# GRU recurrence on TensorE: single-pass products of split operands in place of fp32 products

## The chip, the cores and the metric

The kernel runs on one core of a Trainium2 chip. The metric is the device time of one execution in microseconds (us). The core's engines work side by side and meet at semaphores: PE (TensorE, matmuls; its weight loads are listed as PEld), DVE (VectorE), ACT (ScalarE), POOL (GpSimd) and SP (SyncE, which issues the DMAs).

## The reference, cut to what matters

The whole program is a GRU over 32 time steps, an attention over its states, a residual, then a scan of 32 Runge-Kutta steps with a quantized feed-forward layer on each state, and a second residual. The change touches the GRU. The state h has 128 rows (the batch) and 256 features; each step adds the recurrent products `h @ W_hh` (256 to 768) to the input products:

```
def cell(h, x):
    gi = x @ W_ih + b_ih
    gh = h @ W_hh + b_hh
    i_r, i_z, i_n = jnp.split(gi, 3, axis=-1)
    h_r, h_z, h_n = jnp.split(gh, 3, axis=-1)
    r = jax.nn.sigmoid(i_r + h_r)
    z = jax.nn.sigmoid(i_z + h_z)
    n = jnp.tanh(i_n + r * h_n)
    h_new = (1.0 - z) * n + z * h
    return (h_new, h_new)
_, hs = jax.lax.scan(cell, initial_state, xs)
```

`hs` then goes through the q, k and v projections of the attention. x is (128, 32, 256), in fp32.

## The kernel before, in words

Everything is held transposed: 256 features are two blocks (k) of 128 partitions, and the 128 batch rows are the columns. A gate of 256 features is two output blocks (m) of 128 partitions, so one gate of one step takes 2 x 2 products of a 128x128 weight block with 128 columns of h.

Each engine has its own program, written out by hand, and runs it in that order. The engines meet at semaphores that count (`wait_ge`, `then_inc`); nothing is planned or reordered by a scheduler.

*TensorE* (function `tensor`, the loop at L328). In step t it waits for the h of the step before (`s_h`), runs the gates r, n and z as fp32 products (L337), 12 matmuls in all, each gate into a PSUM bank of its own with a semaphore at its end, and then up to five units of side work (`bulk_unit`, L287 to L315): three units of the input products of the next pair of steps ("gi") and two of the q and k projections of the pair before ("qk"). Side work is done for two steps at once, so it has 256 columns. It uses split operands: a value v is held as a rounded part `v_hi` in the type F32R and a remainder `v_lo = v - v_hi` in the same type, and a product is the sum of three: (lo, hi), (hi, lo) and (hi, hi), two k blocks each, six matmuls a unit (L312 to L314). The six input units of steps 0 and 1 are plain fp32.

*DVE* (function `vector`, L859 to L913), in each step: adds the input part to r (L881), multiplies n's product by the sigmoid of r (L885), adds n's input part (L889), adds z's (L891), forms z*h (L893) and (1-z)*n (L895), and adds these to the new h (L899, semaphore `s_h`). Then it moves the two finished qk units out of PSUM (L856) and rounds one step of x for later input products (L913).

*ACT* (function `scalar`, L634 to L649): sigmoid of r, tanh, sigmoid of z and of -z, up to three outputs of finished gi units, and at the end of the step the rounded part `h_hi` of the new h (L649, semaphore `s_hi`). *POOL* (function `gpsimd`, L1203 to L1216): copies h into the history `hb` that the attention reads (L1208), forms `h_lo` for the qk units (L1211, semaphore `s_hlo`) and `x_lo` (L1215).

The new h alternates between two buffers (`g_h`), h_hi and h_lo between two pairs of steps. The GRU's weights W_hh lie in `wrk` (`whh_s`), loaded in three parts, one per gate. Before the first matmul of the program and in other places `keep_warm` runs matmuls whose results are not used.

Of the kernel before, what the change touches and what calls it, by code (L numbers as in the profile page):

```python
# [6 lines left out]
F32 = mybir.dt.float32  # L7
# [3 lines left out]
ALU = mybir.AluOpType  # L11
# [32 lines left out]
def build(nc, xT, condT, wih, whh, bih, bhh, wq, wk, wv, wo, bqkvo, coupT, cbias, wgT, wuT, wdT, out):  # L44
# [16 lines left out]
    with ExitStack() as ctx:  # L61
        def sb(name, shape, dt=F32):
            return ctx.enter_context(nc.sbuf_tensor(name, shape, dt))

        def sem(name):
# [21 lines left out]
        wmean = sb("wmean", [128, 4])  # L87
        wscale = sb("wscale", [128, 4])
        mag = sb("mag", [128, 2])
        big = sb("big", [128, 8256])  # L90

        kp = lambda d: d.rearrange("(k p) n -> p k n", p=128)
        halves = lambda a: a.rearrange("p (k n) -> p k n", k=2)
# [30 lines left out]
        v_hi, v_lo = ([cut(at, 1024), cut(at + 2048, 1024)] for at in (0, 1024))  # L124
        wv_hi, wv_lo, wo_hi, wo_lo = cut(5120, 512), cut(5632, 512), cut(8192, 512), cut(8704, 512)
        f_hi, f_lo = ([a] * 7 + [b] for a, b in ((cut(6144, 1024), v_hi[0]), (cut(7168, 1024), v_lo[0])))
        Vs = [big[:, 1024 * r:1024 * (r + 1)].rearrange("p (g n) -> p g n", g=4) for r in range(2)]
        PT = [big[:, 2048 + 2048 * r:4096 + 2048 * r].rearrange("p (u n) -> p u n", u=16) for r in range(2)]
        Sc, Sm, Ee, Pn = (big[:, 6144 + 512 * i:6656 + 512 * i].rearrange("p (u n) -> p u n", u=16)
                          for i in range(4))  # L130
        mx, sm, ri = (big[:, 8192 + 16 * i:8208 + 16 * i] for i in range(3))
        banks = PS[:, 0:4, :].rearrange("p g n -> p (g n)").rearrange("p (u n) -> p u n", u=16)
        feats = [PS[:, 5:7, :]] * 7 + [PS[:, 3:5, :]]
        bc = lambda v: v.rearrange("p (u o) -> p u o", o=1).broadcast_to([128, 16, 32])
# [63 lines left out]
        s_r, s_n, s_z = sem("s_r"), sem("s_n"), sem("s_z")  # L198
        s_ar, s_u, s_v, s_az, s_a, s_h = (sem(n) for n in ("s_ar", "s_u", "s_v", "s_az", "s_a", "s_h"))
        s_sr, s_tn, s_sz, s_so = sem("s_sr"), sem("s_tn"), sem("s_sz"), sem("s_so")  # L200
        s_hi, s_hb, s_hlo, s_hlo31 = sem("s_hi"), sem("s_hb"), sem("s_hlo"), sem("s_hlo31")
# [84 lines left out]
        def tensor(pe):  # L286
# [38 lines left out]
            for u in first:  # L325
                bulk_unit(u)
            pe.wait_ge(ld_cond, 16)
            for t in range(T):  # L328
                hprev = g_h[(t - 1) % 2] if t else cond
                if t:  # L330
                    pe.wait_ge(s_h, t)
                for bank, m0, done in ((0, 0, s_r), (1, 4, s_n), (2, 2, s_z)):
                    if t == 0:
                        pe.wait_ge(ld_whh[m0 // 2], 16)
                    for m in range(2):
                        for k in range(2):
                            r = pe.matmul(PS[:, bank, m * 128:(m + 1) * 128],  # L337
                                          whh_s[:, k, (m0 + m) * 128:(m0 + m + 1) * 128], hprev[:, k, :],
                                          start=k == 0, stop=k == 1)
                    r.then_inc(done, 1)  # L340
                for u in at_step[t]:
                    bulk_unit(u)

# [3 lines left out]
            for u in last:  # L347
# [7 lines left out]
            pe.wait_ge(s_hlo, T - 1)  # L355
            pe.wait_ge(s_hlo31, 1)
            for u in last:
                w, m = divmod(u[2], 2)
                for k in range(2):
# [262 lines left out]
        def scalar(ac):  # L622
# [6 lines left out]

            ac.wait_ge(s_const, 1)  # L630
            ac.activation(wsum[:, 3:4], ones[:, 0:1], ACT.Sigmoid)
            for u in first:
                gi_out(u)
            for t in range(T):  # L634
                gis = [u for u in at_step[t] if u[0] == "gi"]
                hn = g_h[t % 2]
                ac.wait_ge(s_ar, t + 1)
                ac.activation(g_r, g_r, ACT.Sigmoid).then_inc(s_sr, 1)  # L638
                ac.wait_ge(s_v, t + 1)
                ac.activation(g_u, g_u, ACT.Tanh).then_inc(s_tn, 1)  # L640
                ac.wait_ge(s_az, t + 1)
                ac.activation(g_z, g_az, ACT.Sigmoid).then_inc(s_sz, 1)
                ac.activation(g_o, g_az, ACT.Sigmoid, scale=-1.0).then_inc(s_so, 1)
                for u in gis[:2]:
                    gi_out(u)
                for u in gis[2:]:
                    gi_out(u)
                ac.wait_ge(s_h, t + 1)
                ac.activation(raw(h_hi[t // 2 % 2][:, :, t % 2 * B:(t % 2 + 1) * B]), hn, ACT.Copy).then_inc(s_hi, 1)  # L649
            ac.wait_ge(s_const, 1)  # L650
            ac.activation(wsum[:, 3:4], ones[:, 0:1], ACT.Exp)
            ac.wait_ge(s_hb, T)
# [181 lines left out]
        def vector(ve):  # L834
# [24 lines left out]
            for t in range(T):  # L859
                n, col = t // 2, t % 2 * B  # L860
                gis = gi[:, n % 2, :, col:col + B]
                hfull = g_h[(t - 1) % 2] if t else cond[:, :, :]
                hn = g_h[t % 2]
                qks = [u for u in at_step[t] if u[0] == "qk"]
                if t == 1:
                    ve.wait_ge(ld_wqk, 32)
                    ve.tensor_copy(raw(wqk_hi), wqk_s).then_inc(s_wqk, 1)
                if t in (2, 3):
                    ve.wait_ge(s_wqk, t - 1)
                    ve.tensor_tensor(raw(wqk_lo[:, t - 2]), wqk_s[:, t - 2], wqk_hi[:, t - 2],  # L870
                                     ALU.subtract).then_inc(s_wqk, 1)
# [24 lines left out]
                if t >= 2:  # L896
                    ve.wait_ge(s_hlo, t - 1)
                ve.wait_ge(s_a, t + 1)
                ve.tensor_tensor(hn, two(g_u), two(g_zh), ALU.add).then_inc(s_h, 1)  # L899
                if t < T - 1:  # L900
                    for u in qks:
                        qk_out(u)
                else:
                    hi, lo = (a[1][:, :, B:2 * B] for a in (h_hi, h_lo))
                    qk_out(qks[0])
                    ve.wait_ge(s_hi, T)
                    ve.tensor_tensor(raw(lo), hn, hi, ALU.subtract).then_inc(s_hlo31, 1)
                    qk_out(qks[1])
# [286 lines left out]
        def gpsimd(po_):  # L1195
# [4 lines left out]
                              pattern=[[-1, 128]], channel_multiplier=1).then_inc(s_const, 1)  # L1200
            po_.wait_ge(s_const, 3)
            po_.tensor_copy(identh[:, :], ident[:, :]).then_inc(s_const, 1)
            for t in range(T):  # L1203
                n, col = t // 2, t % 2 * B
                hn = g_h[t % 2]
                hi, lo = (a[n % 2][:, :, col:col + B] for a in (h_hi, h_lo))
                po_.wait_ge(s_h, t + 1)
                po_.tensor_copy(hb[:, :, :, t], hn).then_inc(s_hb, 1)  # L1208
                if t < T - 1:
                    po_.wait_ge(s_hi, t + 1)  # L1210
                    po_.tensor_tensor(raw(lo), hn, hi, ALU.subtract).then_inc(s_hlo, 1)  # L1211
                if n < 14:
                    at = (n + 2) * 256 + col
                    po_.wait_ge(s_xhi, t + 1)
                    po_.tensor_tensor(raw(x_lo[n % 2][:, :, col:col + B]), x_s[:, :, at:at + B],  # L1215
                                      x_hi[n % 2][:, :, col:col + B], ALU.subtract).then_inc(s_xlo, 1)  # L1216

            po_.wait_ge(s_hlo31, 1)
            po_.wait_ge(s_hlo, T - 1)
# [104 lines left out]
```

## Time and profile before

| | |
|---|---|
| median of 2 runs | 633.4 us (632.79 to 634.02) |
| profiled execution | 632.75 us, of which the span of the trace is 630.8 us |
| PE busy over the span | 590.7 us (94%) |
| PE weight loads (PEld) | 523.7 us (83%) |
| DVE busy | 526.6 us (83%) |
| ACT busy | 404.2 us (64%) |
| POOL busy | 261.5 us (41%) |
| granted TensorE clock | full in all 40 slices of the span |
| recurrent products L337, PE | 744 records of 88.4 us busy, and 24 more with the first state |
| side work L314 of the GRU, split operands, PE | 900 records, 115.6 us busy |

The GRU takes about the first third of the span, the attention the stretch to about 317 us, the scan the rest. A "record" is one TensorE instruction of the trace. Matmuls overlap and their ends are modelled, so the length of one record is longer than the distance between two starts; the cost of one in a dense row is the length of the row divided by the records in it, or the growth of the row with each record. A PE row's "idle before" names who ended the idle time.

### The profile page before, as it was taken

What the parts mean: (1) busy time and instruction counts of PE and PEld (TensorE: products, weight loads), DVE (VectorE), ACT (ScalarE), POOL (GpSimd) and SP (SyncE); (2) the same over time, 40 slices, a digit from 0 to 9 for tenths busy, and PEclk for the clock granted to TensorE, in tenths of its full rate; (3) what the DMA queues carried; (4) which work ended last, traced back from release to release, by engine and by line L of the source; (5) the groups of instructions that cost most, each with busy time, mean ns of one, the idle gap of its engine ahead of it and who ended that gap; (6) DMA issues with size and microseconds to landing.
All of it is one profiled execution on the core that took longest, in us unless ns stands there. A gap on an engine that the chain in (4) does not pass through costs nothing.

```text
span 630.8 us, 14210 instructions
## 1 busy us (share of the span) xinstructions
PE 590.7 (94%) x4918; PEld 523.7 (83%) x4918; DVE 526.6 (83%) x1544; ACT 404.2 (64%) x968; POOL 261.5 (41%) x401
## 2 busy tenths in 40 slices
PE   8899999999999889898879999999999999999997
PEld 7899999999999788787767778777777777777775
DVE  3777777677777588889889999999999999999996
ACT  2554545454544564674467887878778778787775
POOL 0423232323231544221344545555555555555540
PEclk9999999999999999999999999999999999999999
DMA  8400000000000001300000000000000000000000
GB/s 267 159 2 2 1 2 2 1 2 2 1 1 1 18 2 64 118 1 2 1 0 3 18 10 18 16 13 17 11 19 17 11 18 17 11 19 9 19 19 33
DMA packets 12518, 14.87 MB, mean 24 GB/s; under 512 B 1633, under 2 KB 10145, under 8 KB 12449
## 3 DMA queue, kind: packets, MB, share of 16 engines
q1 hardware_dynamic: 12448, 13.97, 6.5%
q8 instruction: 40, 0.66, 0.4%
q14 instruction: 30, 0.24, 0.1%
HBM read 9.78 MB, written 4.19 MB: 22 GB/s over the span
## 4 chain that ended last, share of the span: by engine, by line
PE 68%; ACT 14%; DVE 12%; issue 3%; SPq 1%; DMA 1%; POOL 0%; ACTq 0%; DVEq 0%
PE PS L452 23%; PE PS L314 16%; PE PS L337 12%; ACT q_s L762 4%; PE PS L506 4%; PE PS L528 3%; PE PS L373 2%; ACT q_s L802 2%; ACT k_s L741 2%; ACT big L673 2%; PE PS L430 2%; PE PS L390 2%; DVE big L942 1%; PE PS L490 1%; PE PS L404 1%
## 5 line engine op out<-in xcount | busy, mean ns | idle before, releaser
L452 PE MATMUL PS<-k_s,h_s 128*128 128x128 f32 x1024 | 163.8, 288 | 8.8 <-ACT k_s L741 2.9
L452 PEld LDWEIGHTS PS<-k_s,h_s 128*128 128x128 f32 x1024 | 131.6, 191 | 32.8 <-DVE PS L1034 10.6
L314 PE MATMUL PS<-part 128*128 128x256 f32 x900 | 115.6, 286 | 0.8 <-issue 0.8
L314 PEld LDWEIGHTS PS<-part 128*128 128x128 f32 x900 | 109.8, 191 | 1.0 <-issue 1.0
L741 ACT ACTIVATE k_s<-h_s 128x128 f32<-128x128 f32 x256 | 71.7, 305 | 36.7 <-DVE h_s L1060 32.9
L337 PE MATMUL PS<-big,wrk 128*128 128x128 f32 x744 | 88.4, 275 | 3.0 <-DVE big L899 3.0
L337 PEld LDWEIGHTS PS<-big,wrk 128*128 128x128 f32 x744 | 85.8, 192 | 3.6 <-DVE big L899 3.6
L1208 POOL COPY h_s<-big 128x256 f32<-128x256 f32 x32 | 21.5, 671 | 131.0 <-DVE big L899 131.0
L452 PE MATMUL PS<-h_s 128*128 128x128 f32 x384 | 74.2, 275 | 0.0
L1060 DVE SCALAR_TENSOR_TENSOR h_s<-PS,h_s 128x128 f32<-128x128 f32 x192 | 52.2, 285 | 10.1 <-PE PS L452 7.6
L452 PEld LDWEIGHTS PS<-h_s 128*128 128x128 f32 x384 | 58.3, 192 | 0.0
L638 ACT ACTIVATE big<-big 128x256 f32<-128x256 f32 x32 | 13.4, 418 | 65.6 <-DVE big L881 65.6
L1054 DVE SCALAR_TENSOR_TENSOR h_s<-PS,h_s 128x256 f32<-128x256 f32 x128 | 53.2, 416 | 1.6 <-ACT PS L746 1.1
L746 ACT ACTIVATE PS<-h_s 128x256 f32<-128x256 f32 x128 | 47.8, 373 | 2.9 <-DVE part L948 2.9
L628 ACT ACTIVATE big<-PS,bg 128x256 f32<-128x256 f32 x96 | 41.0, 466 | 6.5 <-DVE bg L838 6.0
L1266 POOL TENSOR_TENSOR h_s<-h_s,k_s 128x256 f32<-128x256 f32 x32 | 25.0, 780 | 42.5 <-DVE q_s L1094 39.7
L1071 DVE SCALAR_TENSOR_TENSOR q_s<-PS,q_s 128x416 f32<-128x416 f32 x64 | 40.8, 640 | 0.6 <-PE PS L554 0.5
L1280 POOL TENSOR_SCALAR h_s<-q_s 128x256 f32<-128x256 f32 x31 | 12.5, 402 | 66.1 <-DVE q_s L1138 66.1
L640 ACT ACTIVATE big<-big 128x256 f32<-128x256 f32 x32 | 13.4, 419 | 38.9 <-DVE big L889 38.9
L1275 POOL TENSOR_TENSOR q_s<-h_s,k_s 128x256 f32<-128x256 f32 x32 | 23.6, 739 | 27.3 <-DVE PS L1040 27.3
L885 DVE SCALAR_TENSOR_TENSOR big<-PS,bh,big 128x128 f32<-128x128 f32 x64 | 19.5, 347 | 18.1 <-ACT big L638 18.1
L762 ACT ACTIVATE q_s<-q_s,mag 128x832 f32<-128x832 f32 x29 | 31.1, 1071 | 0.0
(184 smaller groups left out, 1280.5 us busy)
## 6 DMA issues: line engine op xcount, KB each, us to landing
out<-q_s SPq DMA_DIRECT2D x32, 128.0 KB, 1.7
x_s<-in_xT SPq DMA_DIRECT2D x14, 256.0 KB, 6.2
k_s<-in_wgT SPq DMA_DIRECT2D x1, 832.0 KB, 5.9
k_s<-in_wuT SPq DMA_DIRECT2D x1, 832.0 KB, 7.6
k_s<-in_wih SPq DMA_DIRECT2D x3, 256.0 KB, 4.6
wrk<-in_whh SPq DMA_DIRECT2D x3, 256.0 KB, 4.5
h_s<-in_wdT SPq DMA_DIRECT2D x1, 768.0 KB, 6.4
x_s<-in_xT SPq DMA_DIRECT2D x4, 128.0 KB, 3.8
```

Of the source, the lines that this page charges most:

```text
L314: r = pe.matmul(p, y, x, start=i == 0, stop=i == len(passes) - 1)
L337: r = pe.matmul(PS[:, bank, m * 128:(m + 1) * 128], whh_s[:, k, (m0 + m) * 128:(m0 + m + 1) * 128], hprev[:, k, :], start=k == 0, stop=k == 1)
L452: return pe.matmul(PS[:, m, 0:128], w, x, start=False, stop=True, skip_group_check=True)
L506: r = pe.matmul(po, hqT[0:pk[k], k, :], wd_q[0:pk[k], k, :], start=k == 0, stop=k == NK - 1)
L628: ac.activation(gi[:, n % 2, m, :], bulk_bank(u), ACT.Identity, bias=bg[:, m:m + 1]).then_inc(s_gi, 1)
L741: ac.activation(cm(th[slot % 2], m), cm(src, m), ACT.Tanh).then_inc(s_th, 1)
L746: ac.activation(sqP, src, ACT.Square, scale=math.sqrt(cube[s])).then_inc(s_sq, 1)
L762: ac.activation(hf[:, 0:NI], hN[i % 2], ACT.Identity, scale=h_at(i, 4), bias=mag[:, 0:1]).then_inc(s_hf, 1)
L1054: ve.scalar_tensor_tensor(w_, sqP, cube[s] * own[s], src, ALU.subtract, ALU.mult).then_inc(s_w, 1)
L1060: ve.scalar_tensor_tensor(dst(m), PS[:, m, 0:128], of_ps[slot % 4], cm(w_, m), ALU.mult, ALU.subtract).then_inc(s_next, 1)
L1071: ve.scalar_tensor_tensor(hN[i % 2][:, at], pg[:, g], q_at(i, 3), sg[:, at], ALU.mult, ALU.mult).then_inc(s_hN, 1)
L1266: po_.tensor_tensor(two(W3), two(u3), I_at(t), ALU.add).then_inc(s_W3, 1)
```

## The change

h and the recurrent weights are now used as parts, like the operands of the side work. The gate products of steps 1 to 31 become, for each of the 2 x 2 blocks, three F32R matmuls with 128 columns: lower weights by upper h, upper weights by upper h (`gate_upper`), and upper weights by lower h (`gate_lower`). PE's order in a step is: upper products of r, upper products of n, a wait for the lower h, lower products of r (then `s_r`), lower products of n (then `s_n`), upper and lower products of z (then `s_z`), the side work. Step 0 keeps its fp32 products with the initial state.

The weight parts have a new buffer `whp`; ACT rounds the upper parts before its first step, POOL subtracts for the lower ones. The upper h is written by DVE with an add of its own in front of the add that writes h; the lower h is a DVE subtraction behind it. The ACT rounding and the POOL subtraction of each step go away, and POOL's history copy waits for the lower h. The attention's buffers, which shared the memory of the GRU's, are laid out anew in `big` and a new buffer `sco`.

```
-        big = sb("big", [128, 8256])
+        big = sb("big", [128, 5120])
+        with nc.sbuf_tensor("whp", [128, 3072], F32) as whp:
+            whh_hi, whh_lo = (whp[:, 1536 * i:1536 * (i + 1)].rearrange("p (k n) -> p k n", k=2) for i in range(2))
+        sco = sb("sco", [128, 3136])
...
-            for t in range(T):
-                hprev = g_h[(t - 1) % 2] if t else cond
-                if t:
-                    pe.wait_ge(s_h, t)
-                for bank, m0, done in ((0, 0, s_r), (1, 4, s_n), (2, 2, s_z)):
...
+            def gate_upper(t, bank, m0):
+                hh = h_hi[(t - 1) // 2 % 2][:, :, (t - 1) % 2 * B:((t - 1) % 2 + 1) * B]
+                if t == 1:
+                    pe.wait_ge(s_wlo[m0 // 2], 1)
+                for m in range(2):
+                    for k in range(2):
+                        for w in (whh_lo, whh_hi):
+                            pe.matmul(PS[:, bank, m * 128:(m + 1) * 128],
+                                      raw(w[:, k, (m0 + m) * 128:(m0 + m + 1) * 128]), raw(hh[:, k, :]),
+                                      start=m == 0 and k == 0 and w is whh_lo, stop=False, skip_group_check=True)
+
+            def gate_lower(t, bank, m0, done):
+                hl = h_lo[(t - 1) // 2 % 2][:, :, (t - 1) % 2 * B:((t - 1) % 2 + 1) * B]
+                for m in range(2):
+                    for k in range(2):
+                        r = pe.matmul(PS[:, bank, m * 128:(m + 1) * 128],
+                                      raw(whh_hi[:, k, (m0 + m) * 128:(m0 + m + 1) * 128]), raw(hl[:, k, :]),
+                                      start=False, stop=k == 1, skip_group_check=True)
+                r.then_inc(done, 1)
+
+            for t in range(T):
+                if t == 0:
+                    first_gates()
+                else:
+                    pe.wait_ge(s_hi, t)
+                    gate_upper(t, 0, 0)
+                    gate_upper(t, 1, 4)
+                    pe.wait_ge(s_hlo, t)
+                    gate_lower(t, 0, 0, s_r)
+                    gate_lower(t, 1, 4, s_n)
+                    gate_upper(t, 2, 2)
+                    gate_lower(t, 2, 2, s_z)
...   (scalar)
+            def upper_weights(i):
+                ac.wait_ge(ld_whh[i], 16)
+                ac.activation(raw(whh_hi[:, :, 256 * i:256 * (i + 1)]), whh_s[:, :, 256 * i:256 * (i + 1)],
+                              ACT.Copy).then_inc(s_whi, 1)
...
-                ac.wait_ge(s_h, t + 1)
-                ac.activation(raw(h_hi[t // 2 % 2][:, :, t % 2 * B:(t % 2 + 1) * B]), hn, ACT.Copy).then_inc(s_hi, 1)
...   (vector)
                 ve.wait_ge(s_a, t + 1)
+                ve.tensor_tensor(raw(hi), two(g_u), two(g_zh), ALU.add).then_inc(s_hi, 1)
                 ve.tensor_tensor(hn, two(g_u), two(g_zh), ALU.add).then_inc(s_h, 1)
...
+                ve.wait_ge(s_hi, t + 1)
+                ve.wait_ge(s_h, t + 1)
+                ve.tensor_tensor(raw(lo), hn, hi, ALU.subtract).then_inc(s_hlo, 1)
+                for u in qks:
+                    qk_out(u)
...   (gpsimd)
+            for j, i in enumerate((0, 2, 1)):
+                po_.wait_ge(s_whi, j + 1)
+                po_.tensor_tensor(raw(whh_lo[:, :, 256 * i:256 * (i + 1)]), whh_s[:, :, 256 * i:256 * (i + 1)],
+                                  whh_hi[:, :, 256 * i:256 * (i + 1)], ALU.subtract).then_inc(s_wlo[i], 1)
...
-                po_.wait_ge(s_h, t + 1)
+                po_.wait_ge(s_hlo, t + 1)
                 po_.tensor_copy(hb[:, :, :, t], hn).then_inc(s_hb, 1)
-                if t < T - 1:
-                    po_.wait_ge(s_hi, t + 1)
-                    po_.tensor_tensor(raw(lo), hn, hi, ALU.subtract).then_inc(s_hlo, 1)
```

## Rows read from the trace of the kernel before

**Rows 1.** Stretch 100 to 150 us: busy us of PE, PEld, DVE, ACT, POOL.

```profile
100.00:150.00 50.00, 50.00 (x432) 50.00 (x432) 35.66 (x88) 23.89 (x64) 15.93 (x24) 1.00 0.01 1
```

**Rows 2.** Chain of waits, 98 to 112 us: start us, us, what.

```profile
99.09 2.68 PE PS L337 x24
101.77 3.59 PE PS L314 x30
```

**Rows 3.** Timeline of a steady step: start us, us, engine, line, tiles, count, idle.

```profile
105.20 2.84 PE L337 MATMUL PS<-big,wrk 128*128 128x128 f32 x24
...
106.36 0.42 DVE L881 TENSOR_TENSOR big<-PS,big 128x256 f32<-128x256 f32 x1 [0.17 <-PE PS L337]
...
108.33 0.42 DVE L891 TENSOR_TENSOR big<-PS,big 128x256 f32<-128x256 f32 x1
...
109.23 0.43 DVE L893 TENSOR_TENSOR big<-big 128x256 f32<-128x256 f32 x1 [0.49 <-ACT big L642]
...
109.58 0.42 DVE L895 TENSOR_TENSOR big<-big 128x256 f32<-128x256 f32 x1
110.10 0.42 DVE L899 TENSOR_TENSOR big<-big 128x256 f32<-128x256 f32 x1
...
110.61 0.41 ACT L649 ACTIVATE part<-big 128x256 fp32r<-128x256 f32 x1
...
111.12 0.74 POOL L1211 TENSOR_TENSOR part<-big,part 128x256 fp32r<-128x256 f32 x1
...
111.47 0.72 PE L337 MATMUL PS<-big,wrk 128*128 128x128 f32 x5
```

**Rows 4.** Timeline of the first two steps, and all adds on r (line L881).

```profile
10.54 2.84 PE L337 MATMUL PS<-cond,wrk 128*128 128x128 f32 x24
...
13.99 0.42 DVE L881 TENSOR_TENSOR big<-PS,big 128x256 f32<-128x256 f32 x1
...
14.45 0.42 ACT L638 ACTIVATE big<-big 128x256 f32<-128x256 f32 x1 [3.23 <-DVE big L881]
...
18.13 2.05 PE L337 MATMUL PS<-big,wrk 128*128 128x128 f32 x16 [1.57 <-DVE big L899]
...
19.40 0.42 DVE L881 TENSOR_TENSOR big<-PS,big 128x256 f32<-128x256 f32 x1
...
L881 DVE TENSOR_TENSOR big<-PS,big x32: 410/425/425, 14.0 to 206.4; 128x256 f32<-128x256 f32 x32
```

**Rows 5.** Weight loads: L410's timeline and durations (min/median/max ns), L314's loads.

```profile
265.28 0.28 PE L410 MATMUL PS<-wsum,ones 128*128 128x1 f32 x2
...
265.17 0.31 PEld L410 LDWEIGHTS PS<-wsum,ones 128*128 128x128 f32 x2
...
L410 PEld LDWEIGHTS PS<-wsum,ones x6: 188/190/192, 265.2 to 287.7; 128*128 128x128 f32 x6
L410 PE MATMUL PS<-wsum,ones x6: 164/207/250, 265.3 to 287.7; 128*128 128x1 f32 x6
...
L314 PEld LDWEIGHTS PS<-part x900: 186/192/192, 14.1 to 208.7; 128*128 128x128 f32 x180
```

**Rows 6.** Transposes, one record each: timeline, then groups with mean ns.

```profile
500.50 0.38 PE L545 MATMUL PS<-ident,x_s 128*128 128x128 f32 x2
...
503.30 0.55 PE L490 MATMUL PS<-identh,q_s 128*128 128x128 f16 x7 [0.35 <-ACT q_s L762]
...
L490 PE MATMUL PS<-identh,q_s 128*128 128x128 f16 x203 | 16.0, 218 | 9.8 <-ACT q_s L762 9.8
...
L545 PE MATMUL PS<-ident,x_s 128*128 128x128 f32 x60 | 11.4, 273 | 0.0
```

**Rows 7.** Timeline of the end of the GRU stage.

```profile
210.16 0.42 DVE L899 TENSOR_TENSOR big<-big 128x256 f32<-128x256 f32 x1
...
210.62 0.42 ACT L649 ACTIVATE part<-big 128x256 fp32r<-128x256 f32 x1 [1.05 <-DVE big L899]
...
211.09 2.17 PE L353 MATMUL PS<-part 128*128 128x256 f32 x16 [0.26 <-ACT part L649]
```

More of the change, by code:

```diff
@@ L126, in build @@
         f_hi, f_lo = ([a] * 7 + [b] for a, b in ((cut(6144, 1024), v_hi[0]), (cut(7168, 1024), v_lo[0])))
[L127 to L131, printed above, removed]
+        Vs = [a.rearrange("p (g n) -> p g n", g=4) for a in (big[:, 0:1024], sco[:, 2048:3072])]
+        PT = [big[:, 1024 + 2048 * r:3072 + 2048 * r].rearrange("p (u n) -> p u n", u=16) for r in range(2)]
+        Sc, Sm, Ee, Pn = (sco[:, 512 * i:512 * (i + 1)].rearrange("p (u n) -> p u n", u=16) for i in range(4))
+        mx, sm, ri = (sco[:, 3072 + 16 * i:3088 + 16 * i] for i in range(3))
         banks = PS[:, 0:4, :].rearrange("p g n -> p (g n)").rearrange("p (u n) -> p u n", u=16)
@@ L200, in build @@
         s_sr, s_tn, s_sz, s_so = sem("s_sr"), sem("s_tn"), sem("s_sz"), sem("s_so")
-        s_hi, s_hb, s_hlo, s_hlo31 = sem("s_hi"), sem("s_hb"), sem("s_hlo"), sem("s_hlo31")
+        s_hi, s_hb, s_hlo = sem("s_hi"), sem("s_hb"), sem("s_hlo")
+        s_whi = sem("s_whi")
+        s_wlo = [sem(f"s_wlo{i}") for i in range(3)]
         s_bulk, s_gi, s_qk, s_qka = sem("s_bulk"), sem("s_gi"), sem("s_qk"), sem("s_qka")
@@ L327, in tensor, with first_gates @@
             pe.wait_ge(ld_cond, 16)
-            for t in range(T):
-                hprev = g_h[(t - 1) % 2] if t else cond
-                if t:
-                    pe.wait_ge(s_h, t)
-                for bank, m0, done in ((0, 0, s_r), (1, 4, s_n), (2, 2, s_z)):
-                    if t == 0:
-                        pe.wait_ge(ld_whh[m0 // 2], 16)
+            gates = ((0, 0, s_r), (1, 4, s_n), (2, 2, s_z))
+            def first_gates():
+                for bank, m0, done in gates:
+                    pe.wait_ge(ld_whh[m0 // 2], 16)
                     for m in range(2):
@@ L337, in tensor @@
                             r = pe.matmul(PS[:, bank, m * 128:(m + 1) * 128],
-                                          whh_s[:, k, (m0 + m) * 128:(m0 + m + 1) * 128], hprev[:, k, :],
+                                          whh_s[:, k, (m0 + m) * 128:(m0 + m + 1) * 128], cond[:, k, :],
                                           start=k == 0, stop=k == 1)
                     r.then_inc(done, 1)
+            def gate_upper(t, bank, m0):
[28 more added lines that the diff above has]
+                    gate_lower(t, 2, 2, s_z)
                 for u in at_step[t]:
@@ L354, in tensor @@
                                   stop=False)
-            pe.wait_ge(s_hlo, T - 1)
-            pe.wait_ge(s_hlo31, 1)
+            pe.wait_ge(s_hlo, T)
             for u in last:
@@ L631, in scalar @@
             ac.activation(wsum[:, 3:4], ones[:, 0:1], ACT.Sigmoid)
+            def upper_weights(i):
+                ac.wait_ge(ld_whh[i], 16)
+                ac.activation(raw(whh_hi[:, :, 256 * i:256 * (i + 1)]), whh_s[:, :, 256 * i:256 * (i + 1)],
+                              ACT.Copy).then_inc(s_whi, 1)
             for u in first:
                 gi_out(u)
+            for i in (0, 2, 1):
+                upper_weights(i)
             for t in range(T):
                 gis = [u for u in at_step[t] if u[0] == "gi"]
-                hn = g_h[t % 2]
                 ac.wait_ge(s_ar, t + 1)
@@ L896, in vector @@
                 if t >= 2:
-                    ve.wait_ge(s_hlo, t - 1)
+                    ve.wait_ge(s_hb, t - 1)
+                hi, lo = (a[n % 2][:, :, col:col + B] for a in (h_hi, h_lo))
                 ve.wait_ge(s_a, t + 1)
+                ve.tensor_tensor(raw(hi), two(g_u), two(g_zh), ALU.add).then_inc(s_hi, 1)
                 ve.tensor_tensor(hn, two(g_u), two(g_zh), ALU.add).then_inc(s_h, 1)
-                if t < T - 1:
[L901 to L908, printed above, removed]
+                ve.wait_ge(s_hi, t + 1)
[3 more added lines that the diff above has]
+                    qk_out(u)
                 if n < 14:
@@ L1205, in gpsimd @@
                 hn = g_h[t % 2]
-                hi, lo = (a[n % 2][:, :, col:col + B] for a in (h_hi, h_lo))
-                po_.wait_ge(s_h, t + 1)
+                po_.wait_ge(s_hlo, t + 1)
                 po_.tensor_copy(hb[:, :, :, t], hn).then_inc(s_hb, 1)
-                if t < T - 1:
-                    po_.wait_ge(s_hi, t + 1)
-                    po_.tensor_tensor(raw(lo), hn, hi, ALU.subtract).then_inc(s_hlo, 1)
                 if n < 14:
@@ L1216, in gpsimd @@
                                       x_hi[n % 2][:, :, col:col + B], ALU.subtract).then_inc(s_xlo, 1)
-            po_.wait_ge(s_hlo31, 1)
-            po_.wait_ge(s_hlo, T - 1)
+            po_.wait_ge(s_hlo, T)
             po_.wait_ge(s_hb, T)
```

## The prediction

> **What bounds the kernel now.** I read the views in this order: busy shares by stretch, the chain of waits inside one GRU step, the timeline of that step, and then the rows that tell what one TensorE record costs. The edit sits in the GRU stage; its 32 steps run from the first add on the r gate at 14.0 us to the last at 206.4 us [rows 4]. In that stage PE is busy 50.00 us of 50.00 while DVE has 35.66 and ACT 23.89 [rows 1]. The chain of waits between 98 and 112 us names nothing but PE: 24 records of the recurrent products in 2.68 us, then 30 records of side work (input and q/k products) in 3.59 us [rows 2]. So a step costs 2.68 + 3.59 = 6.27 us, which is also the distance from 105.20 to 111.47, two starts of the recurrent group [rows 3]. A record costs 2.68 / 24 = 0.112 us there and 3.59 / 30 = 0.120 us in the side work.
>
> How much room is beside PE? The last add writes h from 110.10 to 110.53 us, PE takes it at 111.47 [rows 3]: 0.94 us of slack. The first steps, whose side work is 18 records and not 30, show the recurrence bare: adds on r at 13.99 and 19.40 us, 5.41 us apart, with PE idle before it starts at 18.13 [rows 4]. The intervals between the 32 adds on r are 2 of 5.41, 28 of 6.27, and the last one, whose side work is 12 records: 192.4 - 10.8 - 175.6 = 6.0 us.
>
> **The change part by part.** *Recurrent products.* Twelve fp32 matmuls a step, recorded as two records each (24), become 36 single products with 128 moving columns: (low weights, high h), (high, high), (high, low h). I expect one record each, since the side work, in the same number format, has 5 units of 6 products and 30 records. Everything hangs on the price p of one such record, and no row of before shows this format at 128 columns. Bounds from the nearest rows:
>
> - The moving pass alone: seven fp16 transposes with 128 columns take 0.55 us, one record 0.218, so 0.33 / 6 = 0.055 us each [rows 6]. That is the low end.
> - The weight load: a fresh 128x128 block precedes every product. Two fp32 products with a single moving column, nothing to stream, still span 0.28 us where the shortest is 0.164, so the second comes 0.112 us after the first; their two loads, 0.188 to 0.192 us long, span 0.31 [rows 5]. Loads of the side work's format have the same length, 192 ns at the median [rows 5]; the fp16 transposes do not pay it. Two fp32 transposes, one record of 0.273 each, span 0.38, so they are 0.11 us apart too [rows 6].
> - The side work's own pace, 0.120 us at 256 columns: the high end of the simple reading, as half the columns should not cost more.
>
> By the load rows p lies between 0.108 and 0.120; I take 0.115, halfway between the one-column pair and the side work, as the format is the side work's and the width is nearer the pair's. The matmul gets half as long and the load does not: three products of one load each in place of two records of one load each. Group time: 36 x 0.115 = 4.14 us against 2.68, so +1.46 us a step, and PE has no idle time in a steady step to absorb it.
>
> The Trainium skill's page "TensorE: Matmul & The Clock Gate" (LDWEIGHTS) gives a load as columns / 1.2 ns, 107 ns for 128, and its table of weight-path modes says that fast weight load has no win for fp32. By that figure alone the step would be 36 x 0.107 = 3.85 us, the forecast 669; the trace's one-column pair stands 5 ns above it.
>
> *Recurrence.* PE now runs high products of r and n (16), waits for the low part of h, runs 4 + 4 low ones, then z. The r gate is complete after 20 records, not 8: 20 x 0.115 - 8 x 0.112 = +1.41 us before the add on r. z is complete after 36 x 0.115 = 4.14 us, plus 0.28 for the last record's length; its add stood at 108.33 - 105.20 = 3.13 us and would be shifted to 4.54 anyway, so z sets nothing. The bare recurrence is 5.41 + 1.41 = 6.82 us, below the 4.14 + 3.59 = 7.73 us of PE: in steady steps PE stays the bound, with about 0.9 us of slack for h.
>
> *New wait for the low part.* PE's wait stands in front of the 20 remaining gate products and all side work of the step. DVE writes the high part where h was written, then h 0.35 us later (the pace of independent adds, 109.23 to 109.58), the low part 0.52 later again (a dependent add, 109.58 to 110.10), and it ends 0.42 after that [rows 3]: 1.29 us after the start of the high add. PE starts on the high part at about 0.5 at the earliest and spends 16 x 0.115 = 1.84 us on it. Covered by 1.0 us, cost nothing; if PE were bound by h and p were 0.055, the cover would still be 0.1 us.
>
> *DVE.* Two more adds a step, some 0.87 us, ahead of the two q/k outputs. DVE has 14.3 of 50 us idle [rows 1], 1.8 us a step. Its outputs wait for PE's side work in any case. *ACT* loses the rounding copy (0.41 us) and *POOL* the low subtraction (0.74 us) [rows 3]; neither was on the chain, so nothing. POOL's copy of h into the history now waits for the low part, about 0.9 us later than before; DVE reuses h two steps on, nothing.
>
> *Splitting the weights.* Three ACT copies of 512 columns, at most twice the 0.42 us of 256 columns each, stand before ACT's first sigmoid. ACT sits idle for the 3.23 us before 14.45, and the last third of the weights has landed by the time PE begins z without a pause, 10.54 + 16 x 0.112 = 12.3 us [rows 4]. 12.3 + 0.84 = 13.2 is before 14.45: hidden. POOL's three subtractions, at most 1.5 us each, end before 18.13, when step 1 begins: hidden.
>
> *Start, end, storage.* Step 0 keeps its fp32 products. After the last step PE started the final q/k products at 211.09, behind ACT's rounding at 210.62; the high part is now there when h was (210.16 + 0.42) [rows 7]: -0.4 us. The moved attention buffers change no instruction: nothing.
>
> *Sum.* 28 steady intervals x 1.46 = 40.9. The other 3 go by the recurrence: 3 x 1.41 = 4.2. End -0.4. Together +44.7 us on the profiled execution's 632.75 us (span 630.8 and 1.95 around it), which lies 0.65 below the median shown: **677 us**, 1.07 times. With p = 0.108 the sum is 28 x 1.21 + 3 x 1.27 - 0.4 = +37.3, 670 us; with 0.120 it is 28 x 1.64 + 3 x 1.51 - 0.4 = +50, 683 us.
>
> **The rivals.** *Loads hide, the change wins* (the other side). If the array takes a block's weights at no cost beside a 128-column pass, p is 0.055 to 0.065 (the pass, plus the 0.008 by which the side work exceeds two such passes). At 0.060 PE needs 2.16 + 3.59 = 5.75 us, the recurrence 5.41 + 1.20 - 0.90 = 5.71: 0.52 us less in 28 steps, 0.3 more in 3, -0.4: 619 us; 614 to 624 over the span of p. It decides at the weight load before each of the 36 products, from p below 2.68 / 36 = 0.0745. For it: the fp16 pace [rows 6]. Against it: the one-column pair [rows 5]. Chance 0.08, half of it beyond 2%. The same page's issue-gap rule, N / 2.4 + 2.5 ns, would give 56 ns a product and this case; the one-column pair speaks against its use here.
>
> *The format loses its advantage at 128 columns* (the change does not do what it says). Each product costs what an fp32 one does now, two records, 0.224 us: 8.06 + 3.59 = 11.65 us, +5.38 in 28 steps. z ends so late that it sets the other 3: its add moves from 3.13 to 8.06 + 0.28 + 0.09 = 8.43, +5.3. 28 x 5.38 + 15.9 - 0.4 = +166, 799 us. For it: all this format's rows have 256 or 512 columns, none 128. Against: nothing in its rows hints at a second pass. Chance 0.12.
>
> *Load and pass do not overlap for short products*: p = 0.107 + 0.065 = 0.172. PE 6.19 + 3.59 = 9.78, +3.51 in 28; the 3 others by z, +3.4: +108, 741 us. For it: the fp32 transposes, whose pace of 0.11 is a short load plus a short pass. Against: the side work, whose 0.120 holds both side by side. Chance 0.08.
>
> **How the numbers follow.** Forecast 0.72, rivals 0.08, 0.12 and 0.08. The forecast's bounds are 670 to 683; I add 4 below for steps whose DVE work now ends sooner relative to PE. The forecast and the non-overlap rival together hold 0.80, so the range is 666 to 745. What a measurement here can tell from no change is about 2%, 621 to 646 us: faster 0.04, within 0.04, slower 0.92.
>
> **What would show it.** In the changed profile: the high and low gate groups with 36 records a step and PE at 100% in steady steps; 7.7 us between adds on r; starts of gate records 0.11 to 0.12 us apart, loads still 190 ns; PE not idle at the wait for the low part; clock at 1.00. A pace near 0.06 and PE idle before each step would prove the first rival, 72 records or 0.22 us per record the second, 0.17 us the third. A stall of PE before the low products would show my cover wrong.

## The result, and the profile after

The changed kernel takes 681.6 us (median of 2 runs, 680.2 to 682.9) against 633.4 (median of 2 runs): slower, ratio 1.076 with a 95% interval of 1.071 to 1.081. Its profiled execution took 680.17 us, with a span of 678.2 against 630.8.

The same stretch as [rows 1], now of the changed kernel; the columns are busy us of PE, PEld, DVE, ACT and POOL:

```profile
100.00:150.00 50.00, 50.00 (x436) 50.00 (x435) 32.81 (x87) 18.65 (x49) 8.42 (x12) 1.00 0.00 1
```

PE is still busy throughout and everything else is less so. The chain of waits of one steady step answers to [rows 2] (start us, us, what; L353 is the line of the products with the upper h, L361 of those with the lower h, L319 the side work):

```profile
120.65 1.74 PE PS L353 x16
122.39 0.89 PE PS L361 x8
123.28 0.90 PE PS L353 x8
124.17 0.45 PE PS L361 x4
124.62 3.63 PE PS L319 x30
```

36 gate records take 3.98 us, 0.111 us each, where 24 took 2.68, and the side work takes 3.63 us where it took 3.59. The step is 7.61 us and holds nothing but PE. The timeline shows the slack beside it, as [rows 3] did:

```profile
119.07 0.43 DVE L940 TENSOR_TENSOR part<-big 128x256 fp32r<-128x256 f32 x1
119.41 0.42 DVE L941 TENSOR_TENSOR big<-big 128x256 f32<-128x256 f32 x1
119.93 0.43 DVE L944 TENSOR_TENSOR part<-big,part 128x256 fp32r<-128x256 f32 x1
...
120.49 1.90 PE L353 MATMUL PS<-part,whp 128*128 128x128 f32 x16
...
122.22 1.05 PE L361 MATMUL PS<-part,whp 128*128 128x128 f32 x8
```

The upper h (L940) is there at 119.50, 0.99 us before PE takes it, and the lower h (L944) at 120.36, 1.86 us before its first product. No steady step waits for a part of h. PE waits for the upper h only in step 1 (2.3 us) and in step 31 (1.1 us), where the side work before it is short; the kernel before waited there too.

What is not in steady steps stands at the start, against [rows 4]:

```profile
11.98 5.49 POOL L1243 TENSOR_TENSOR whp<-wrk,whp 128x512 fp32r<-128x512 f32 x3 [10.01 <-ACT whp L670]
12.23 2.83 DVE L887 TENSOR_TENSOR part<-k_s,part 128x1536 fp32r<-128x1536 f32 x1
14.99 0.41 DVE L921 TENSOR_TENSOR big<-PS,big 128x256 f32<-128x256 f32 x1
...
16.60 1.15 DVE L929 TENSOR_TENSOR big<-big 128x256 f32<-128x256 f32 x1
...
22.86 0.42 DVE L921 TENSOR_TENSOR big<-PS,big 128x256 f32<-128x256 f32 x1 [0.94 <-PE PS L361]
31.73 0.42 DVE L921 TENSOR_TENSOR big<-PS,big 128x256 f32<-128x256 f32 x1 [1.45 <-PE PS L361]
```

The first add on r comes 1.0 us late, and the first two steps last 7.87 and 8.87 us. In the second, the clock is low; the columns of the next row are as above, then PE's granted clock:

```profile
21.65:28.47 6.82, 6.82 (x34) 6.82 (x34) 3.48 (x10) 2.03 (x5) 0.85 (x1) 0.50 0.05 15
```

Half clock is the 1.2 GHz level. The 20 gate records from 21.70 to 25.96 us start 0.213 us apart, against 0.111 at full clock. Before it PE had been busy only 4.14 of the 6.60 us from 15.00 on. A second such stretch runs from 250.3 to 257.2 us, at the end of the GRU stage.

All adds on r run from 15.0 to 252.0 us:

```profile
L921 DVE TENSOR_TENSOR big<-PS,big x32: 412/425/425, 15.0 to 252.0; 128x256 f32<-128x256 f32 x32
```

**Where the 47.4 us of span are.** Start +1.0; the first two intervals 16.74 against 10.82, +5.9; the 28 steady ones 28 x (7.60 - 6.27) = +37.2; the last 7.42 against 5.99, +1.4; behind the last add 426.2 against 424.4, +1.9.

### The profile page after: what moved, and what is told of

Same layout as the page of the kernel before. It is cut to its first block, busy times and chain, and to the rows that moved or that the text cites. A ratio compares the mean times of both kernels' runs of the same rounds, so it can differ in the third digit from the quotient of the medians.

```text
span 678.2 us, 14992 instructions
## 1 busy us (share of the span) xinstructions
PE 637.7 (94%) x5290; PEld 571.0 (84%) x5290; DVE 543.9 (80%) x1607; ACT 395.9 (58%) x939; POOL 249.0 (37%) x373
## 4 chain that ended last, share of the span: by engine, by line
PE 73%; ACT 13%; DVE 8%; issue 3%; SPq 1%; DMA 1%; POOL 0%; ACTq 0%; DVEq 0%
PE PS L488 21%; PE PS L319 16%; PE PS L353 12%; PE PS L361 6%; ACT q_s L802 4%; PE PS L542 4%; PE PS L564 3%; ACT q_s L842 2%; ACT k_s L781 2%; PE PS L466 2%; PE PS L409 2%; PE PS L426 2%; ACT sco L713 2%; DVE big L980 1%; PE PS L526 1%
## 5 line engine op out<-in xcount | busy, mean ns | idle before, releaser
L319 PE MATMUL PS<-part 128*128 128x256 f32 x900 | 116.4, 287 | 1.6 <-issue 1.6
L319 PEld LDWEIGHTS PS<-part 128*128 128x128 f32 x900 | 111.7, 194 | 1.8 <-issue 1.8
L353 PE MATMUL PS<-part,whp 128*128 128x128 f32 x744 | 93.8, 276 | 3.4 <-DVE part L940 3.4
L353 PEld LDWEIGHTS PS<-part,whp 128*128 128x128 f32 x744 | 90.1, 195 | 3.8 <-DVE part L940 3.8
L361 PE MATMUL PS<-part,whp 128*128 128x128 f32 x372 | 54.2, 283 | 0.0
L361 PEld LDWEIGHTS PS<-part,whp 128*128 128x128 f32 x372 | 49.1, 201 | 0.0
L921 DVE TENSOR_TENSOR big<-PS,big 128x256 f32<-128x256 f32 x32 | 13.6, 425 | 40.3 <-PE PS L361 40.3
```

The source lines that it names most:

```text
L319: r = pe.matmul(p, y, x, start=i == 0, stop=i == len(passes) - 1)
L353: pe.matmul(PS[:, bank, m * 128:(m + 1) * 128], raw(w[:, k, (m0 + m) * 128:(m0 + m + 1) * 128]), raw(hh[:, k, :]), start=m == 0 and k == 0 ...
L361: r = pe.matmul(PS[:, bank, m * 128:(m + 1) * 128], raw(whh_hi[:, k, (m0 + m) * 128:(m0 + m + 1) * 128]), raw(hl[:, k, :]), start=False, s ...
```

## The experiments

All are edits of the changed kernel, and ratios are to the kernel before. Where one experiment's change is built on another's, it says so.

**Is it the load or the pass?** Two runs halve the one and the other. The pass is the streaming of the columns of h, the load is that of the weight block. In the first run each gate product streams 64 columns of h, so half of the batch is left out of the gates:

```
-   pe.matmul(PS[:, bank, m * 128:(m + 1) * 128], raw(w[:, k, ...128 columns]), raw(hh[:, k, :]), ...
+   pe.matmul(PS[:, bank, m * 128:m * 128 + 64],  raw(w[:, k, ...128 columns]), raw(hh[:, k, 0:64]), ...
```

> The 36 gate products of each step stream 64 columns of h in place of 128 (half of the batch's gates are left out); weight blocks, order and waits stay. Theory L (each product pays the load of a fresh 128x128 block, 0.11 us, which the pass of 128 columns hides behind): the records stay 0.111 us apart, a steady step stays at 7.6 us, the time near 680 us (678 to 683). Rival P (at 128 columns the format streams twice, like the fp32 transposes, 2 x 0.055 us): the pace falls to about 0.06, PE needs 36 x 0.06 + 3.63 = 5.8 us, a step 5.7 to 5.9, the time about 627 to 633 us.

Measured: 706.2 us, one execution. Chain of waits of one step:

```profile
117.92 1.71 PE PS L353 x16
119.62 0.89 PE PS L361 x8
120.52 0.89 PE PS L353 x8
121.41 0.45 PE PS L361 x4
```

36 records in 3.94 us, 0.109 each: half the streaming bought nothing, and the steps at full clock stay at 7.61 us. Rival P is out. The time was missed for another reason, which neither theory had: the clock. The next rows are the stretch with these lines and the one after it:

```profile
112.00:122.00 10.00, 10.00 (x89) 10.00 (x89) 6.21 (x17) 3.10 (x8) 1.41 (x2) 1.00 0.00 0
122.20:125.60 3.40, 3.40 (x18) 3.40 (x18) 2.30 (x7) 1.99 (x6) 0.34 (x1) 0.50 0.02 5
```

PE is listed as busy for all of both, with records in the first as dense as in the changed kernel, and yet the grant drops to half for 3.4 us again and again through the GRU stage; the 11 steps in which it does last 9.1 us. Before that it was at half from 19.8 to 43.7 us, and the first three intervals lasted 9.6, 11.5 and 11.3 us. Together these are 24.5 of the 26.0 us by which the span is longer than the changed kernel's. That the narrower pass is what lowers the clock is argued from this one execution; no other run tests it.

In the second run the weight blocks have 64 columns, so half of each gate's outputs are left out, and 128 columns of h pass:

```
-   pe.matmul(PS[:, bank, ...],     raw(w[:, k, (m0 + m) * 128:(m0 + m + 1) * 128]),  raw(hh[:, k, :]), ...
+   pe.matmul(PS[0:64, bank, ...],  raw(w[:, k, (m0 + m) * 128:(m0 + m) * 128 + 64]), raw(hh[:, k, :]), ...
```

> The 36 gate products load weight blocks of 64 columns in place of 128 (half of each gate's outputs are left out) and stream 128 columns of h as in the changed kernel. Theory L: the load halves to about 0.053 us and the pace falls to 0.056 to 0.065 us, a steady step to 5.7 to 5.9 us, the time to about 627 to 633 us. Rival P: the two passes stay, 0.11 us a record, the time near 680 us.

Measured: 636.3 us, one execution. Durations of loads and products (min/median/max ns), and one step:

```profile
L361 PEld LDWEIGHTS PS<-part,whp x372: 133/135/223, 22.1 to 209.4; 128*64 128x64 f32 x186
...
114.66 1.12 PE L353 MATMUL PS<-part,whp 128*64 128x128 f32 x16
...
115.27 1.23 DVE L896 TENSOR_SCALAR k_s<-PS,ba 128x256 f32<-128x256 f32 x2
...
116.33 0.29 DVE L951 CAST part<-x_s 128x256 fp32r<-128x256 f32 x1
...
116.53 0.42 DVE L921 TENSOR_TENSOR big<-PS,big 128x256 f32<-128x256 f32 x1
...
116.71 0.73 POOL L1253 TENSOR_TENSOR part<-x_s,part 128x256 fp32r<-128x256 f32 x1 [0.55 <-DVE part L951]
...
117.58 3.83 PE L319 MATMUL PS<-part 128*128 128x256 f32 x30 [0.59 <-POOL part L1253]
```

The load is 57 ns shorter than the changed kernel's 192, and 16 products take 1.12 - 0.22 = 0.90 us beyond one record's length, 0.06 us each. With the passes untouched, the price per product falls with the load: theory L holds. By columns / 1.2 ns, the Trainium skill, "TensorE: Matmul & The Clock Gate" (LDWEIGHTS), gives 53 ns for a load of 64 columns and 107 for one of 128. The trace agrees with the difference, 57 ns between the loads' records. The pace of 0.06 us is also near that of a pass of 128 columns (0.055, [rows 6]), so it shows that the shorter load costs no more than this, not what it costs by itself.

My time for this run was too low by 3 to 9 us. The step is 6.2 us, not 5.8. I took the cause for POOL: lower h, two q/k outputs, cast of x, POOL's lower x, and only then the side work, before which PE idles 0.59 us; the expectations of the first three fp16 versions below still say so. The chain of waits of this run says otherwise: it holds neither PE nor POOL and goes on DVE from the lower h (L944) over the two q/k outputs (L896, 1.23 us) and the cast (L951) straight to the next add on r (L921), then on between DVE and ACT.

**Is it the number of products?** One of three products is left out, and with it POOL's subtractions:

```
-   for w in (whh_lo, whh_hi):
+   for w in (whh_hi,):
...
-   po_.tensor_tensor(raw(whh_lo[...]), whh_s[...], whh_hi[...], ALU.subtract)
```

> Two products per block and step in place of three (lower weights by upper h is left out), and POOL's three subtractions for the lower weights at the start are gone with it. Theory L: 24 records x 0.111 = 2.67 us, so a step is 2.67 + 3.6 = 6.27 us again: 28 x -1.33 = -37 us and about -4 in the first and last steps; without POOL's subtractions the first add on r is back at 14.0 us and DVE's adds of step 0 at 0.42 us, -1.7. Together 636 to 641 us. Rival W (what costs is the wait for the lower h or the two added DVE operations, not the number of records): a steady step stays above 7 us and the time above 665 us.

Measured: 635.4 us, ratio 1.003 (1.001 to 1.005), 0.6 us below what I expected. One step's gate products in its chain of waits, and of its start the long subtraction and two adds:

```profile
103.21 0.84 PE PS L353 x8
104.05 0.90 PE PS L361 x8
104.95 0.45 PE PS L353 x4
105.39 0.45 PE PS L361 x4
```

```profile
12.45 1.75 DVE L887 TENSOR_TENSOR part<-k_s,part 128x1536 fp32r<-128x1536 f32 x1
14.12 0.41 DVE L921 TENSOR_TENSOR big<-PS,big 128x256 f32<-128x256 f32 x1
...
15.85 0.42 DVE L929 TENSOR_TENSOR big<-big 128x256 f32<-128x256 f32 x1
```

24 records, 2.64 us, and 6.26 us a step: the price of the fp32 version, although the wait for the lower h and DVE's two added operations are all there. (The profile is of the longest of the five executions, 640.5 us; its stretches at half clock lie outside the rows shown.) Rival W is out. DVE's start is back to its old durations once POOL's subtractions are gone.

**One part undone.** The gate products go back to fp32 on h; the rest of the change stays:

```
-   pe.wait_ge(s_hi, t)
-   gate_upper(t, 0, 0)
...
+   pe.wait_ge(s_h, t)
+   (the 12 fp32 products of the kernel before)
```

> The changed kernel with the gate products of steps 1 to 31 put back to fp32 on h itself; everything else of the change stays (DVE writes both parts, POOL and ACT lose theirs, the weights are still split at the start, the attention's buffers stay moved). Theory L: a steady step is 24 x 0.112 + 3.6 = 6.27 us again; what is left is the start, where POOL's subtractions slow DVE (1.0 us before the first add on r, 0.7 in step 0) and perhaps a lower clock in the first steps: 634 to 639 us, ratio to the kernel before 1.002 to 1.008. Rival W: the added DVE operations hold the steps above 6.6 us, 645 us or more.

Measured: 638.4 us, ratio 1.0065 (1.0048 to 1.0082), within what was expected. The chain of waits of a step is that of before:

```profile
100.11 3.59 PE PS L319 x30
103.71 2.68 PE PS L374 x24
```

So of the 7.6% the gate products are 7, and the rest of the change, the start included, is 0.65%.

**The slow start.** POOL starts its subtractions behind DVE's long one:

```
+   po_.wait_ge(s_wih, 2)
    for j, i in enumerate((0, 2, 1)):
        po_.wait_ge(s_whi, j + 1)
```

> The changed kernel, but POOL begins its three subtractions for the lower recurrent weights only when DVE has done its long subtraction for the input weights. Theory S (two-input operations of POOL and DVE that run at the same time slow each other: DVE's subtraction took 2.83 us beside them, 1.75 alone): DVE's subtraction is back at 1.75 us and the first add on r at 13.9 to 14.2 us; the collision moves into step 0, whose adds beside POOL take 0.7 to 1.1 us in place of 0.42, so the total stays within 2 us of the changed kernel's. Rival T (DVE was slow for another reason, the placement of the buffers): 2.8 us and a first add at 15 us as before.

Measured: 682.0 us (2 runs, ratio 1.078, 1.072 to 1.084), as expected. Its start:

```profile
12.56 1.75 DVE L887 TENSOR_TENSOR part<-k_s,part 128x1536 fp32r<-128x1536 f32 x1
14.23 0.42 DVE L921 TENSOR_TENSOR big<-PS,big 128x256 f32<-128x256 f32 x1
14.40 3.95 POOL L1244 TENSOR_TENSOR whp<-wrk,whp 128x512 fp32r<-128x512 f32 x3 [12.43 <-DVE part L887]
...
15.85 1.38 DVE L929 TENSOR_TENSOR big<-big 128x256 f32<-128x256 f32 x1
17.14 0.41 DVE L931 TENSOR_TENSOR big<-PS,big 128x256 f32<-128x256 f32 x1
```

The long subtraction is back at 1.75 us and the collision has moved to L929, 1.38 us in place of 0.42. L931, which has one operand in PSUM, ran at 0.41 while POOL was at work, and so did L921 in the changed kernel. That fits the Trainium skill, "SBUF — State Buffer" (SBUF: two separate sides): DVE and GpSimd have one port pair in common, and the instruction that starts first holds it alone. The traces agree on the order too. In the changed kernel POOL began first (11.98 against 12.23 us) and DVE's long subtraction grew by 1.08 us. In the run with filled idle time, next, DVE began first, kept its 1.75 us beside POOL, and POOL's three took 4.99 us in place of 3.95:

```profile
12.13 1.75 DVE L896 TENSOR_TENSOR part<-k_s,part 128x1536 fp32r<-128x1536 f32 x1
12.71 4.99 POOL L1252 TENSOR_TENSOR whp<-wrk,whp 128x512 fp32r<-128x512 f32 x3 [10.74 <-ACT whp L679]
```

The runs show the slowdown only between operations that have both inputs in SBUF. The first add on r came 0.76 us earlier than in the changed kernel, but the total gained nothing: the second interval was 9.25 us (8.87), and 428.1 us (426.2) passed behind the last add, with a stretch at half clock from 325.5 us among them. So what the start costs is read from the rows, not from a time.

**The clock.** Unused matmuls fill PE's idle time in steps 0 and 30:

```
    for u in at_step[t]: bulk_unit(u)
+   if t == 0:
+       pe.wait_ge(s_ar, 1)
+       keep_warm(0, 9)
+   if t == T - 2:
+       pe.wait_ge(s_ar, T - 1)
+       keep_warm(0, 8)
```

(and six more ahead of step 0's side work)

> The changed kernel with unused matmuls where PE sits idle: 12 records before and 18 behind the side work of step 0, 16 behind that of step 30. Theory C: the granted clock of one half that the changed kernel shows for 6.8 us from 21.6 us and again from 250.3 us comes from the idle PE just before (3.9 us in step 0, some 2 us each in steps 30 and 31) and costs about 2 us each time; filled, the first steps cost 6.8 us, not 8.9, and the time is 676 to 679 us, ratio to the changed kernel about 0.994. Rival D: the lower clock comes from the sparser recurrent products themselves (128 columns for each load), and it stays: 680 to 683 us.

Measured: 678.8 us (674.5 to 680.5), ratio 1.070 (1.065 to 1.075), at the upper edge of theory C's range; its interval overlaps that of the changed kernel. The two stretches that were low before are now whole in the profiled execution, and the second interval is 6.7 us, not 8.9:

```profile
20.00:32.00 12.00, 11.73 (x102) 11.53 (x102) 7.88 (x20) 4.25 (x12) 3.08 (x4) 1.00 0.19 68
240.00:260.00 20.00, 18.86 (x180) 18.56 (x179) 12.84 (x30) 6.84 (x14) 6.57 (x6) 1.00 0.05 15
```

In the profile the direction is shown: the 12 us from 20.00 hold 102 records and not 79. That execution was the fastest of the four, the only one with a mean granted clock of 1.000; the others had 0.995 to 0.997, still above the 0.990 and 0.985 of the changed kernel's two. In the times it is not settled, and what the filling cost elsewhere (the first interval grew to 8.3 us) was not taken apart.

**A version with a cheap load.** If a rounded 32-bit block costs 0.11 us and an fp16 transpose with 128 columns goes at 0.055, the same three products in fp16 parts should be cheap. h, and the recurrent and q/k weights, as fp16 pairs:

```
-   with nc.sbuf_tensor("whp", [128, 3072], F32) as whp:
+   with nc.sbuf_tensor("whp", [128, 3072], FP16) as whp:
...
-   ve.tensor_tensor(raw(hi), two(g_u), two(g_zh), ALU.add).then_inc(s_hi, 1)
+   ve.tensor_tensor(hi, two(g_u), two(g_zh), ALU.add).then_inc(s_hi, 1)
```

> The changed kernel with h and the weights it meets (recurrent, q and k) split into two fp16 parts, not two of the rounded 32-bit format; three products a block as before, same order; the input products keep their format. Theory L: fp16 blocks load in far less than 0.11 us, so a gate product costs 0.056 us and a q/k product 0.109. PE: 36 x 0.056 + 12 x 0.109 + 18 x 0.12 = 5.5 us a step, but the chain that set 6.18 us in the run with half blocks (lower h, q/k outputs, cast of x, POOL's lower x, input products) is as long: steps of 6.0 to 6.2 us, 627 to 633 us. Rival P (128 columns are too short for three products in any format): 0.1 us and more a product, 675 us and up.

Measured: 632.0 us (10 runs), ratio 0.997 (0.996 to 0.999), inside the expected range; the steps are 6.1 us. With x in fp16 parts too:

> As the fp16 version for h, with x and its weights in fp16 parts as well: all 66 products of a step are fp16. Theory L: PE needs 36 x 0.056 + 30 x 0.109 = 5.3 us a step and waits; the chain over POOL's lower x sets the step at 5.9 to 6.1 us: 624 to 630 us. Rival: a step bound by PE would gain the full 0.3 us against the other fp16 version.

Measured: 632.7 us, ratio 0.998 (0.996 to 1.000), above the expected range by 2.7 us, and the steps are 6.1 us again. The cheaper side work brought nothing, so PE is no longer the bound; but my account of what is was not right, as the next one shows. It is built on the version with all products in fp16: the cast of x and POOL's lower x were moved ahead (and the unused matmuls were in):

> All products in fp16 parts, the unused matmuls in steps 0 and 30, and the cast of x moved ahead of DVE's last operations of the step, with POOL's lower x ahead of its history copy. Theory X: what holds the light steps is the chain lower h, q/k outputs, cast of x, lower x, input products; moved out of it, the step falls to the recurrence, 5.41 + 20 x 0.056 - 0.90 = 5.63 us: 28 x -0.64 = -18 us against the kernel before, 615 to 620 us. Rival Y: the added adds on DVE bound the step, and it stays at 6.0 us or more, 626 us and up.

Measured: 635.4 us, ratio 1.003 (1.002 to 1.004). Theory X fell: the cast and POOL's lower x had left the chain, and the step was 6.2 us all the same; rival Y's 626 us and more came true. Its timeline names the cause:

```profile
114.45 1.07 PE L355 MATMUL PS<-p,whp 128*128 128x128 f16 x16 [0.79 <-DVE p L956]
114.83 0.42 DVE L960 TENSOR_TENSOR p<-big,p 128x256 f16<-128x256 f32 x1
115.17 1.16 DVE L907 TENSOR_SCALAR k_s<-PS,ba 128x256 f32<-128x256 f32 x2
...
115.35 0.61 PE L363 MATMUL PS<-p,whp 128*128 128x128 f16 x8
...
116.18 0.40 DVE L932 TENSOR_TENSOR big<-PS,big 128x256 f32<-128x256 f32 x1
...
118.82 0.67 POOL L1262 TENSOR_TENSOR p<-x_s,p 128x256 f16<-128x256 f32 x1 [2.83 <-DVE p L947]
...
119.02 0.75 DVE L949 TENSOR_TENSOR big<-big 128x256 f32<-128x256 f32 x1 [0.28 <-ACT big L695]
```

r's last product, the fourth of the eight from 115.35, ends at about 115.8, but DVE is in the two q/k outputs and gets to the add on r at 116.18. The move also had a price: POOL's lower x now runs beside DVE's z*h (L949), which takes 0.75 us in place of 0.42 (median of 31), 0.33 us a step on the chain. So this run does not show what taking the cast off the chain (0.28 us) is worth; without the collision its step would still be about 5.9 us, an estimate from 6.25 - 0.33, and not theory X's 5.63.

In the PE-bound kernels the outputs lay in DVE's idle time. Now, again from the version with all products in fp16 and without the unused matmuls, they go one step later, one behind the add on r and one behind the add on z, where DVE waits for a sigmoid:

```
    ve.tensor_tensor(two(g_r), two(PR), gis[:, 0:2], ALU.add).then_inc(s_ar, 1)
+   for u in qks[:1]: qk_out(u)
...
+   for u in qks[1:]: qk_out(u)
    ve.wait_ge(s_sz, t + 1)
...
-   for u in qks: qk_out(u)          (behind the lower h)
```

> All products in fp16 parts; the two q/k outputs of a step are taken by DVE one step later, one behind the add on r and one behind the add on z, where DVE waits for ACT's sigmoids, and not behind the lower h; POOL forms the lower x before its history copy. Theory Y (from the run with the cast of x moved: DVE's operations in front of the next add on r, 1.16 us of q/k outputs among them, set the light step): the add on r comes when PE has r, 0.35 us earlier, and a steady step falls from 6.1 - 6.2 to 5.7 - 5.9 us; 28 x -0.45 = -13 us against the kernel before, 1.5 to 3 back for the start: 621 to 626 us. Rival Z (the recurrence itself is 6.1 us long once the parts are formed): no gain against the other fp16 versions, 630 to 634 us.

Measured: 615.3 us (614.5 to 618.8), ratio 0.972 (0.969 to 0.976), 6 us under my range. The add on r again waits for PE:

```profile
115.55 1.07 PE L355 MATMUL PS<-p,whp 128*128 128x128 f16 x16 [0.15 <-DVE p L946]
...
116.45 0.61 PE L363 MATMUL PS<-p,whp 128*128 128x128 f16 x8
...
116.95 0.42 DVE L923 TENSOR_TENSOR big<-PS,big 128x256 f32<-128x256 f32 x1 [0.39 <-PE PS L363]
```

16 products in 1.07 us are (1.07 - 0.22) / 15 = 0.057 each, and the steps are 5.61 us. The two q/k outputs (0.66 us each) end within 0.13 us of the sigmoids for which DVE would wait anyway. The formula of the prediction's first rival, 5.41 + 20 x 0.056 - 0.90, gives 5.63. This is faster than both kernels.

> The same with the unused matmuls in steps 0 and 30. Both theories: the granted clock is full in the GRU stage either way in most runs, so the two differ by less than 2 us; if the version without them shows a stretch at half clock, this one is 1 to 2 us faster.

Measured: 617.7 us, ratio 0.974 (0.971 to 0.977). Its interval overlaps that of the version without the filling, so the filling is worth nothing that shows here.

## Why the prediction was right, and where its terms were off

- **PE is the bound and has no room.** Right: the chain of waits of a steady step is PE alone before and after, and the run with fewer products took back in full what they had cost.
- **The price of a product, the load.** Right in kind, 4% too high in size. I took 0.115 us, halfway between the one-column pair [rows 5] and the side work; it is 0.111, near the pair's 0.112. Over 28 steps that is 40.9 us forecast against 37.2. But I had misread the pair. Its second product starts 0.026 us after the first, not 0.112, and is the longer one (0.250 us after 0.164), so it is their ends that lie 0.112 apart, and their loads start 0.118 apart (265.167 and 265.285 us). The pair pointed at the load, but its nearness to 0.111 is in part luck. The load's part, which I could only argue from it, is shown by the two half runs.
- **Side work, wait for the lower h, slack.** Right: 3.63 us where I had 3.59, in a steady step PE never waits for a part, 0.99 us of slack where I had 0.9.
- **DVE's two adds cost nothing.** Right in this kernel, and shown by the run with two products. It held only under PE's cover: in the light versions DVE's queue was the bound (6.1 us, and 5.61 with the q/k outputs moved). What the two adds alone cost there was not measured.
- **The three intervals by the recurrence.** The working is right, its conditions were not: +4.2 us forecast, +7.4 measured. With the clock whole the second interval was 6.70 us (the run with filled idle time), where 5.41 + 1.41 = 6.82 was forecast. In the changed kernel it was 8.87, about 2.2 us lost at half clock. The first lost 0.7 us to L929 and 0.4 to its four lower products of r at half clock, 4 x (0.213 - 0.111). I had expected the clock at 1.00 throughout.
- **The weights' splitting is hidden.** Wrong: +1.0 us before the first add and 0.7 in step 0. I checked that ACT and POOL were free in time, which they were, but not what POOL's work does to DVE beside it. This is the one term that was put at nothing on a wrong reason; the later start of POOL showed it.
- **The end.** -0.4 us forecast, +1.9 measured: PE came late to the last q/k products, 259.19 us, 1.7 us behind the upper h at 257.50, behind side work and unused matmuls that the half clock had delayed. With the clock whole, in the run with filled idle time, the stretch behind the last add was 423.7 us, -0.7 against the kernel before.
- **The rivals.** Hidden loads: out, but its arithmetic came true for a format with a cheap load. The issue-gap rule that I cited with it (the Trainium skill, "TensorE: Matmul & The Clock Gate", Back-to-back issue gap) is given there for an isolated product, beside about 81 ns for a stream of loads and products of 128 columns; this case shows 111 ns with 32-bit blocks and 57 with fp16 ones. Two passes at 128 columns: out, by 36 records a step and not 72, and by the half weights at 0.06. No overlap of load and pass (0.172): out, at 0.111.

The sum was only 2.7 us too low, and that is luck: the 28 steady intervals were forecast 3.7 us too high, and the start, the three intervals and the end together 6.5 too low.

## What to carry to other kernels

Price a TensorE product as the larger of two paces, that of its pass and that of its weight load, and take each from a record of the same format and width: where every product brings a fresh block of 32-bit weights and streams 128 columns or fewer, fewer columns save nothing and a third product costs a third load. At 256 columns the two paces are close, and the product cost a little more than either (0.120 us, against 0.111 here and 0.109 in fp16), so there a row of its own is needed. When a change swaps one operand format for another, ask first which of the two paces it moves; fp16 pairs moved the one that bound here. And once the bound engine is light, read the in-order queue of the next one again: work that was free beside a busy PE, here two outputs in front of the next step's first add, becomes the step.

## What the runs showed of the hardware that was not expected

- The granted clock fell although the trace lists PE as busy without a gap: with 64 columns streamed per gate product it was at half for 3.4 us at a time (0.90 on average from 100 to 150 us), with 128 columns and as many gate records a step it stayed at 1.00. One execution; the cause is open.
- PE's records at half clock, loads of 128 columns among them, started 0.213 us apart against 0.111.
- DVE operations with both inputs in SBUF ran 1.6 to 3.3 times as long when POOL's two-input subtractions were already under way (1.75 to 2.83 us, 0.42 to 1.38); begun before POOL's, the long one kept its 1.75 us and POOL's were longer. Those with an input in PSUM were not slowed.
- The rounded 32-bit format takes 0.120 us a product at 256 columns, where fp16 takes 0.109 at the same width (medians over the side work of the changed kernel and of the versions with all products in fp16).
